# Layers 1 and 2 of a recommendation tower: 128 columns of weights in one matmul, or four tiles of 32 columns

## The reference

```
z = einsum('bke,kef,bkf->bk', e[:, I], W, e[:, J])     # 780 pairs, 32 x 32 each
h = concatenate([z, dense_ctx], axis=1)                # 796
h = maximum(h @ W_top1 + b_top1, 0)                    # 796 x 512
h = maximum(h @ W_top2 + b_top2, 0)                    # 512 x 256
y = h @ W_top3                                         # 256 x 1
```

## Time and profile before

| what | us |
|---|---|
| device time, median of 3 runs | 634.8 |
| lowest and highest run | 633.32, 635.27 |
| span of the profiled execution, first to last instruction | 1130.1 |
| TensorE busy in it | 875.4 |
| VectorE busy in it | 540.3 |
| ScalarE busy in it | 327.1 |

### The profile page before, as it was taken

One profiled execution on the slowest core, in us unless ns is written; L12 is line 12 of the kernel. 1 busy time (PEld: TensorE's weight loads), 2 busy tenths in 40 slices (PEclk: granted clock), 3 DMA queues, 4 the chain that ended last, 5 costly groups with the idle time before them and its releaser, 6 DMA issues.

```text
span 1130.1 us, 16792 instructions
## 1 busy us (share of the span) xinstructions
PE 875.4 (77%) x7232; PEld 201.8 (18%) x7232; DVE 540.3 (48%) x510; ACT 327.1 (29%) x243; POOL 412.3 (36%) x436
## 2 busy tenths in 40 slices
PE   4322358788779995886895789779889787899998
PEld 1000012121112220121121112112112111122223
DVE  3100067364345660452380447337245264688884
ACT  4001047553246380032260134127244000000002
POOL 6777341533353137324517151451624604000000
PEclk8555598887578895886796788989779788899999
DMA  4100044201001020100101002010010102011010
GB/s 155 32 14 13 12 145 127 63 7 52 9 11 53 12 72 13 44 16 18 38 22 41 5 10 75 9 47 4 12 34 8 39 3 58 8 39 29 1 36 3
DMA packets 30489, 39.24 MB, mean 35 GB/s; under 512 B 11376, under 2 KB 19200, under 8 KB 30160
## 3 DMA queue, kind: packets, MB, share of 16 engines
q1 hardware_dynamic: 14880, 25.59, 7.7%
q0 software_dynamic: 13824, 7.11, 4.3%
q10 hardware_dynamic: 1712, 5.48, 1.4%
HBM read 21.93 MB, written 0.07 MB: 19 GB/s over the span
## 4 chain that ended last, share of the span: by engine, by line
PE 65%; another core or an unknown queue 17%; issue 11%; DVE 3%; ACT 2%; SPq 1%; DMA 1%; DVEq 0%; ACTq 0%
PE t_ps L857 27%; PE z_ps L881 18%; PE x_ps L898 10%; PE x_ps L806 7%; PE x_ps L911 2%; SPq L543 1%; DVE prod L727 1%; ACT one_hot L602 1%; PE t_ps L911 1%; DVE one_hot L689 1%; PE t_ps L898 1%; PE t_ps L829 0%; DVE z_sb L673 0%; ACT one_hot L605 0%
## 5 line engine op out<-in xcount | busy, mean ns | idle before, releaser
L727 DVE TENSOR_TENSOR prod<-t_ps,e_t 128x1024 f32<-128x1024 f32 x392 | 459.4, 1213 | 425.2 <-remote 300.6
L558 POOL DMA_INDIRECT rows<-cold_tables,idx x432 | 412.1, 954 | 550.1 <-DVE e_t L734 420.2
L857 PE MATMUL t_ps<-e_t,w_sb 32*64 32x512 f32 x3120 | 362.0, 658 | 73.8 <-issue 53.6
L881 PE MATMUL z_ps<-prod,select 128*32 128x512 f32 x1560 | 243.5, 639 | 21.7 <-issue 21.0
L602 ACT ACTIVATE one_hot<-hot_sb,row_number 128x2048 bf16<-128x2048 f16 (+1 forms) x75 | 140.6, 1875 | 110.3 <-remote 87.4
L898 PE MATMUL x_ps<-z_sb,w_sb 128*32 128x512 f32 x704 | 131.1, 635 | 24.4 <-issue 22.5
L605 ACT ACTIVATE one_hot<-one_hot 128x2048 bf16<-128x2048 bf16 (+1 forms) x75 | 134.3, 1791 | 2.4
L857 PEld LDWEIGHTS t_ps<-e_t,w_sb 32*64 32x64 f32 x3120 | 74.6, 136 | 323.0 <-issue 221.6
L806 PE MATMUL x_ps<-one_hot,tables 128*32 128x512 bf16 x1194 | 97.8, 402 | 27.3 <-issue 22.6
L806 PE MATMUL t_ps<-one_hot,tables 128*32 128x512 bf16 x198 | 45.3, 501 | 92.1 <-issue 87.9
L689 DVE TENSOR_SCALAR one_hot<-hot_sb,row_number 128x2048 bf16<-128x2048 f16 (+1 forms) x47 | 33.9, 744 | 133.2 <-remote 130.0
(11 more groups left out here) (33 smaller groups left out, 98.6 us busy)
## 6 DMA issues: line engine op xcount, KB each, us to landing
e_t<-e_t SPq DMA_DIRECT2D x64, 128.0 KB
e_t<-e_t SPq DMA_DIRECT2D x112, 64.0 KB
rows<-cold_tables,idx POOLq DMA_INDIRECT x432
hot_sb<-hot_ids SPq DMA_DIRECT2D x11, 512.0 KB, 3.6
w_sb<-w_lay ACTq DMA_DIRECT2D x1, 1792.0 KB, 7.0
z_sb<-hot_tables SPq DMA_DIRECT2D x4, 320.0 KB, 5.1
w_sb<-w_lay ACTq DMA_DIRECT2D x1, 1216.0 KB
w_sb<-w_lay ACTq DMA_DIRECT2D x1, 896.0 KB, 4.6
```

The source lines that it names most:

```text
L558: pool.indirect_dma_start(out=rows[:, slot, span, :], out_offset=None, in_=table, in_offset=bass.IndirectOffsetOnAxis(ap=idx[:, n, span:sp ...
L727: nc.vector.tensor_tensor(prod[:, u % PROD_SLOTS, 0:banks, :], t_ps[:, at:at + banks, :], by, ALU.mult).then_inc(mult_done, 1)
L857: mm = nc.tensor.matmul(t_ps[cols, at + n, :], w_sb[part, b, cols], e_t[part, e_slot(k, of[side]), :], start=True, stop=True)
L881: mm = nc.tensor.matmul(z_ps[E * q:E * q + E, :], select[:, E - PER - PER * s:2 * E - PER - PER * s], prod[:, (u + q // 2) % PROD_SLOTS, q ...
```

## The change

The loops over `q` in `layer1` and `layer2` are gone. One matmul takes all 128 columns of weights and writes all 128 partitions of the bank. The moving operand, the waits, the counts and the order of the steps are as they were. A step becomes two loads and two passes.

```diff
@@ layer1
                 into = bank_of(use)
-                for q in range(PER):
-                    mm = nc.tensor.matmul(into[E * q:E * q + E, :], w1_sb[:, kb, m * P + E * q:m * P + E * q + E],
-                                          z_sb[:, bank % Z_RING, :], start=first, stop=ends)
+                mm = nc.tensor.matmul(into, w1_sb[:, kb, m * P:m * P + P], z_sb[:, bank % Z_RING, :],
+                                      start=first, stop=ends)
                 if ends:
                     mm.then_inc(x_made, 1)
@@ layer2
                 into = bank_of(use)
-                for q in range(PER):
-                    mm = nc.tensor.matmul(into[E * q:E * q + E, :], w2_sb[:, j, m * P + E * q:m * P + E * q + E],
-                                          h1_sb[:, j, :], start=first, stop=ends)
+                mm = nc.tensor.matmul(into, w2_sb[:, j, m * P:m * P + P], h1_sb[:, j, :], start=first, stop=ends)
                 if ends:
                     mm.then_inc(x_made, 1)
```

## The result

| what | us |
|---|---|
| before, median of 4 runs | 634.32 (633.32 to 635.27) |
| changed kernel, median of 4 runs | 648.10 (647.66 to 649.71) |
| ratio | 1.0233, 95% interval 1.0214 to 1.0252 |
| profiled execution of the changed kernel: its time, its span | 648.48, 646.5 |

The changed kernel is slower by 2.33%, which is 14.8 us of 634.3 (13.6 to 16.0); the two medians lie 13.8 us apart. The forecast was 648.0.

The account below looks back on a forecast made before the run. TensorE was taken as the bound nearly throughout, its steps adding up to 592 of 634.8 us with 43 left over. Changes of shape add 13.2 us: 634.8 + 13.2 = 648.0 us, own range 644.3 to 651.9, 8-in-10 range 636 to 662.

Parts of the forecast that it names:

- TensorE is the bound, and its loss shows in full: Whole kernel: TensorE's steps make 592 of 634.8 us, so what it gains or loses shows in full.
- Rival D: Supply of instructions: if the unexplained 43 us were stalls, 1536 fewer records give back 4.6 us; 643.4 us, chance 0.07.
- Streaming costs the same, fewer instructions are worth nothing: Layers 1 and 2: only 0.02 us of stagger per visit saved; 1536 fewer loads and passes beside a full array save nothing.
- The load of the second pass is hidden: Within a layer step: the second pass's load lies under the pass before it, taken as zero; other end 0.172 us each.
- rival B: The 128-column float32 load is not hidden under the pass before it: 28.7 us more, 676.7 us, chance 0.07.
- Changes of shape: Layers 1 and 2 stop sharing red's shape 128*32, giving separate visits: +13.2 us, with bounds +9.5 and +17.1.
- Rival A: No emptying between shapes of equal rows; only 58 entries from a gen pay the longer load, 3.7 us: 638.5, chance 0.08.
- rival C: Only tiled work has to be emptied, borders with the full array are free: -7.5 us, 627.3 us, chance 0.06.
- The size of a visit: An unbroken run of 128*128 steps adds 0.18 us beyond its passes, bounds 0.138 and 0.223.
- The sum: Layer runs: 65 x 0.18 = 11.7, 22 x 0.042 = 0.9, 2 x (0.18 + 0.138) = 0.6; together +13.2 us.
- VectorE: It has slack, products some 2.44 us per gen against 2.9 for a gen with other steps; nothing taken off.
- Rival E: VectorE covers half: if the timed run waits for products far oftener, half of 13.2 us is hidden; 641.4, chance 0.07.

Follow-up runs that it names:

- the profile without gaps: The kernel before, unchanged, profiled again: it took 633.53 us, with a span of 631.5 us.
- 128*64: Layers 1 and 2 multiply with two tiles of 64 columns side by side, where the kernel before has four tiles; ratio 1.0164, +10.4 us.
- the regrouped order: Kernel before, layer steps moved in 29 places to the next gap between gens: 646.62 us, ratio 1.0206; the changed kernel so reordered: 656.03 us, ratio 1.0355.

## Why the prediction was right, point by point

- *TensorE is the bound, and its loss shows in full.* Right. TensorE's busy time grew by 14.8 us and the span by 15.0. Of the 43 us that the sum of steps left over, less belongs to the start than I had thought: the first gen stands at 34.6 us in the profile without gaps, but 258 look-up records ahead of it, 14.0 us at the price of the sum, are in the sum already, so 20.6 are left. Then come 7.2 us in 21 gens that take too long, 2.0 us between span and time (633.53 - 631.5), and look-ups: the 1134 records behind the first gen take 75.6 us, where the sum has 61.4 for them and some 5 more for their borders with gens. The last few us are not accounted for. Rival D lived on stalls as in rows 2, and this profile has none.
- *Streaming costs the same, fewer instructions are worth nothing.* Right: 0.430 us a pass at the end of after, 0.43 before.
- *The load of the second pass is hidden.* Right, and with it rival B is out: the second of two steps adds 0.85 us. The rule of the Trainium skill ("TensorE: Matmul & The Clock Gate", Part 3) by which loads overlap only with passes of another row group does not hold for the runs here: loads of 128 rows lie under passes of the same 128 rows, with 32, 64 and 128 columns.
- *Changes of shape.* Right, and this term decides. 128*32 and 128*128 are different shapes: red ahead of layer 1 went from 0.86 to 1.00. The rule of the Trainium skill ("TensorEngine Tiling (Array Packing)", Key Properties) that a change of the tiling mode drains TensorE agrees with what this pair and 128*64 show, 0.09 us a border beside the load. Rival A, with free borders between shapes of 128 rows, and rival C are out by the same rows.
- *The size of a visit.* 0.18 was forecast, 0.198 measured. This term was too small by 0.018 us a visit. The load takes 190 ns and not 172: I had taken the rate per column from a load of 64 columns with 32 rows (131 ns); one of 64 columns with 128 rows takes 136, so the rate is 27 per 32 columns and not 22.
- *The sum.* With 0.198 the sum is 65 x 0.198 + 22 x 0.060 + 2 x (0.198 + 0.138) = 14.9 us, beside 14.8 by the ratio and 13.8 by the medians. That the forecast of 648.0 met the median of 648.10 to 0.1 us is luck: 13.2 is 1.6 us short of 14.8, the base of 634.8 was 0.5 us above the median of four runs, and the four runs of either kernel lie 2 us apart.
- *VectorE.* I took nothing off for gaps in which VectorE is late. That was right for this change: the same 21 gens are too long in after as before, 7.2 us in both, so no part of the 14.9 was covered. Rival E is out. But the slack is thinner than I had thought: the regrouped order lost 13.0 us on it.

The visit costs by shape, in one table. The stagger is what four or two tiles start apart (0.020 and 0.007 us, from the starts of their passes); what is left falls on one line, 0.09 us and 0.027 us for each 32 columns of the first load.

| shape of the visit | cost over the passes, us | less stagger |
|---|---|---|
| 128*32, four tiles | 0.138 | 0.118 |
| 128*64, two tiles | 0.151 | 0.144 |
| 128*128 | 0.198 | 0.198 |

The two parts can also be read directly from the starts of the passes, in visits of one step. From the first pass to the second of the same tile it is 0.453, 0.480 and 0.534 us for 32, 64 and 128 columns, where passes in a row are 0.429 apart: that is the bare part of the first load, 0.024, 0.051 and 0.105. From the second pass to the first of the next shape it is 0.543, 0.529 and 0.522, and without the stagger 0.52 each time: 0.09 more than a pass. And a red between a gen and a look-up, which has red's shape but bf16 in place of float32, takes 0.882 in place of 0.996, less by the 0.09 and the stagger: the 0.09 comes with a change of shape, not with one of step or type. The runs show it as a constant of the border and don't show what the array does in it. Which of the two shapes at a border it belongs to is not told apart either.

No version beat the kernel before. The experiments point to none with wider matmuls: each of them makes borders or lengthens a first load. They point to the waits for VectorE, 6.4 of the 7.2 us. 14 of these 20 gens lie among the first 46, where there is no layer step yet to fill the gap, so layer steps can't mend their 4.7 us; the six others lose 1.7 us together. Moving a step there might be worth 1 us, an estimate, which these runs can't tell from nothing, and it was not tried.

## What to carry to other kernels

Four matmuls of 32 columns side by side on one moving operand were no slower here than one of 128, 0.858 us a step either way: the passes stream together, and the loads lie under them. Ask instead what shape the neighbours on TensorE have: each visit to a shape cost 0.14 to 0.20 us here beyond its passes, and only steps of one shape in a row share it, so count the unbroken runs, not the steps. And where an engine is ahead of another by a few tenths of a microsecond in each period, the order in which filler steps are spread over the periods counts: the same steps in another order cost 13.0 us.

## What the runs showed that I had not expected

- One profiled execution of the kernel had a span of 1130.1 us, with gaps of 1.4 us between records of TensorE, while its timed runs and a second profile are at 634 and 631.5. What held it up is not shown. A step's cost taken from a stretch without gaps was good to 0.01 us all the same.
- The length of a float32 load of 128 rows is 109, 136 and 190 ns for 32, 64 and 128 columns: 27 ns for each 32 columns and a constant of 82. Bare, at the head of a visit, only the part that grows with the columns shows (0.11 us of the 0.19 with 128 columns in after); the 0.09 us of the exit is the same for all three widths.
- The three-unit buffer between TensorE and VectorE did not carry 0.37 us from one gap to the next.
